# One loading order changed on SyncE: all four quarters of w1 issued right behind the picks

## The reference, cut to what matters

```python
e = stack([tbl_f[ids[:, f]] for f in range(32)], axis=1)      # (512, 32, 32)
x0 = prev = e
for W in (filter_0, filter_1):                                # (1, 32*32, 128), (1, 32*128, 128)
    z = einsum('bhd,bmd->bhmd', x0, prev).reshape(512, h * m, 32)
    prev = relu(einsum('bpd,pn->bnd', z, W[0])); outs.append(prev)
z = sum(concatenate(outs, axis=1), axis=-1)                   # (512, 256)
h = concatenate([z, dense_ctx], axis=1)                       # (512, 272)
h = maximum(h @ W_top1 + b_top1, 0)
h = maximum(h @ W_top2 + b_top2, 0)
y = h @ W_top3                                                # (512, 1)
```

## Time and profile before

| | |
|---|---|
| median of 3 runs | 834.16 us (834.12 to 834.23) |
| the profiled execution | 833.78 us |
| its span (first to last instruction) | 832.0 us |
| PE busy | 825.9 us (99%) |
| ACT busy | 795.8 us (96%) |
| DVE busy | 789.3 us (95%) |
| POOL busy | 731.0 us (88%) |

### The profile page before, as it was taken

One profiled execution on the slowest core, in us unless ns is written; L12 is line 12 of the kernel. 1 busy time (PEld: TensorE's weight loads), 2 busy tenths in 40 slices (PEclk: granted clock), 3 DMA queues, 4 the chain that ended last, 5 costly groups with the idle time before them and its releaser, 6 DMA issues.

```text
span 832.0 us, 15690 instructions
## 1 busy us (share of the span) xinstructions
PE 825.9 (99%) x3627; PEld 677.7 (81%) x3627; DVE 789.3 (95%) x2061; ACT 795.8 (96%) x2808; POOL 731.0 (88%) x550
## 2 busy tenths in 40 slices
PE   8999999999999999999999999999999999999999
PEld 6688888888888888888888888888888888888887
DVE  7799999999999999999999999999999999999996
ACT  4799999999999999999999999999999999999995
POOL 5898999989999999999999999999999999999860
PEclk9999999999999999999999999999999999999999
DMA  5541222221233221132331132221122222122000
GB/s 149 180 143 32 66 81 85 86 85 36 63 82 84 84 86 47 51 85 82 84 87 49 48 87 80 84 86 55 43 87 80 86 85 68 33 83 78 1 13 2
DMA packets 62024, 60.91 MB, mean 73 GB/s; under 512 B 26059, under 2 KB 36939, under 8 KB 61934
## 3 DMA queue, kind: packets, MB, share of 16 engines
q1 hardware_dynamic: 57838, 57.80, 23.4%
q0 software_dynamic: 4096, 2.11, 1.6%
HBM read 55.51 MB, written 4.31 MB: 72 GB/s over the span
## 4 chain that ended last, share of the span: by engine, by line
PE 97%; DMA 1%; POOL 1%; issue 0%; SPq 0%; DVE 0%; ACT 0%
PE ps_y L915 28%; PE ps_y L923 28%; PE ps_y L916 28%; PE ps_c L898 3%; PE ps_c L897 3%; PE ps_c L896 3%; POOL gat L452 1%; PE ps_c L894 1%; DMA w_raw<-w 1%; PE ps_c L885 0%; DMA gat<-table,rows 0%; PE ps_y L1019 0%; DMA ids_and_bounds_sb<-ids_and_bounds 0%; POOL w_lo L459 0%; PE ps_y L1021 0%
## 5 line engine op out<-in xcount | busy, mean ns | idle before, releaser
L571 ACT ACTIVATE prod<-ps_y,es 128x128 f32<-128x128 f32 x2560 | 754.1, 647 | 15.8 <-PE ps_y L923 15.6
L740 DVE SCALAR_TENSOR_TENSOR prod<-ps_y,es,prod 128x128 f32<-128x128 f32 x1536 | 422.6, 340 | 28.7 <-PE ps_y L923 26.4
L915 PE MATMUL ps_y<-w_hi,c_both 128*128 128x512 f32 x1024 | 402.8, 393 | 1.0 <-POOL w_lo L459 1.0
L923 PE MATMUL ps_y<-w_hi,c_both 128*128 128x512 f32 x1024 | 398.8, 390 | 0.0
L916 PE MATMUL ps_y<-w_lo,c_both 128*128 128x512 f32 x1024 | 398.6, 389 | 0.0
L441 POOL TENSOR_TENSOR prod<-prod 128x768 f32<-128x768 f32 x128 | 247.1, 1931 | 45.9 <-DVE prod L740 34.2
L752 DVE TENSOR_REDUCE csum<-prod 128x64 f32<-128x896 f32 x256 | 276.5, 1081 | 0.1
L916 PEld LDWEIGHTS ps_y<-w_lo,c_both 128*128 128x128 f32 x1024 | 192.4, 188 | 43.2 <-issue 1.0
L915 PEld LDWEIGHTS ps_y<-w_hi,c_both 128*128 128x128 f32 x1024 | 192.5, 188 | 42.9 <-issue 2.8
L923 PEld LDWEIGHTS ps_y<-w_hi,c_both 128*128 128x128 f32 x1024 | 192.2, 188 | 41.4
L431 POOL TENSOR_TENSOR z<-first,second 128x512 f32<-128x512 f32 x155 | 199.7, 1299 | 0.1
(11 more groups left out here) (122 smaller groups left out, 295.7 us busy)
## 6 DMA issues: line engine op xcount, KB each, us to landing
second<-et_scratch SPq DMA_DIRECT2D x155, 256.0 KB, 4.8
first<-et_scratch SPq DMA_DIRECT2D x31, 256.0 KB, 3.2
et_scratch<-gat SPq DMA_DIRECT2D x62, 64.0 KB
w_raw<-w SPq DMA_DIRECT2D x4, 512.0 KB, 4.7
h_scratch<-h_sums SPq DMA_DIRECT2D x120, 2.0 KB
gat<-table,rows_now POOLq DMA_INDIRECT x116, 2.4
wt_sb<-wt SPq DMA_DIRECT2D x2, 512.0 KB
rows_now<-rows SPq DMA_DIRECT2D x29, 2.0 KB, 1.7
```

The source lines that it names most:

```text
L571: last = nc.scalar.activation(prod[:, buffer_of(g, u), place // 2, :, place % 2], ps_y[:, bank_of(g, u, k), j * N:(j + 1) * N], ACT.Copy, ...
L740: last = nc.vector.scalar_tensor_tensor(out=summed, in0=ps_y[:, bank_of(g, u, k), j * N:(j + 1) * N], scalar=es[:, g.r, u, h:h + 1], in1=s ...
L915: nc.tensor.matmul(out, hi, w_hi, start=True, stop=False)
L923: nc.tensor.matmul(out, lo, w_hi, start=False, stop=True).then_inc(y_ready, 1)
```

## The change

SP no longer waits for the gathers of group 0. It issues quarters 0 to 3 of `w1` one behind the other right behind the picks. The quarter 3 that stood between the writes and the reads of group 1 is gone from there. The same DMAs are issued in all.

```diff
@@ -317,12 +317,10 @@
             sp.dma_start(w0b_sb, w0b).then_inc(w0_in, 16)
             sp.dma_start(copy_sb[:, :], copy_of).then_inc(w0_in, 16)
             sp.dma_start(picks_sb[:, :, :], picks).then_inc(picks_in, 16)
-            filters(0)
+            for n in range(W1_LOADS):
+                filters(n)
             for s in range(SLOTS):
                 sp.sem_inc(h1_written[s], 16 * BT)
-            sp.wait_ge(gathered[0], 16 * TG)
-            for n in range(1, W1_LOADS - 1):
-                filters(n)
 
             def stage(g):
 
@@ -359,7 +357,6 @@
 
             send(Group(0, 1))
-            filters(W1_LOADS - 1)
             fetch(Group(0, 1))
```

## The result

The change made the kernel slower: 837.53 us in the median of 16 runs (835.41 to 845.12) against 833.96 for the kernel before (833.63 to 834.36, 16 runs). The ratio is 1.0051, with a 95% interval of 1.0032 to 1.0069. The median lies 0.5 us above the range of the prediction (833.7 to 837.0), and what was forecast was +0.8 us, no measurable change. Every ratio in this document leaves out runs in a slower state; only the run at 846.94 us, in one of the experiments, was such a run.

| mean granted clock | runs | us |
|---|---|---|
| 1.000 | 3 | 835.41 to 836.01 |
| 0.997 and 0.998 | 8 | 836.80 to 837.80 |
| 0.996 | 3 | 838.24 to 838.56 |
| 0.994 | 2 | 845.02 and 845.12 |

What follows compares the result with a forecast made beforehand. The prediction took one long PE stream and its start to bound the kernel. Gathers later by 2.0 us less 1.17 us for the removed wait gave +0.8 us, 835.0 us in the median, range 833.7 to 837.0.

Steps and rivals of the forecast that it cites:

- What bounds the kernel: Whole span: one long PE stream with a start in front; moving the start or opening a hole moves the end equally.
- Removed: ACT's wait for quarter 3: At banks 6 and 7 of `w1`: ACT and POOL come sooner, PE's hole shrinks to 0.2 us; gain 1.17 us.
- Moved: 1.5 MB of traffic, onto the gathers: Before the picks: group 0's fourth gather lands at 12.6 instead of 10.6 us, a cost of 2.0 us.
- the round robin: Group 0's gathers, rival: they pass between the quarters, waiting for one packet only; sum -0.3 to -1.2 us, chance 15%.
- my rule: Group 0's gathers: one behind quarters lands when they are through, 0.1 us before the last to 0.6 behind it.
- PE's clock falls in the longer pause: Rival, between warm-up and picks: a 3.6 us pause drops the clock, +2.0 us more, 837.0 us; chance 20%.

Runs made afterwards that it cites:

- the run at 846.94 us: Kernel before with only quarter 3 moved, and DVE instead of POOL making bank 6's `w_lo`: median 839.60 us, ratio 1.0043; the profiled run took 846.94.
- the kernels with quarter 3 moved and the gap: Kernel before with quarter 3 moved, POOL waiting for DVE before its first folds: 833.59 us; with DVE taking bank 6, 833.11; with POOL's `w_lo` held back, 833.48.
- the kernel with one quarter fewer: Kernel before with quarters 0 to 2 issued right behind the picks and quarter 3 behind group 0's gathers: 836.24 us, ratio 1.0012.

## Why the prediction was wrong, point by point

*What bounds the kernel* was right: all of the loss in the profile arises in the first 31 us (+4.70) and is carried to the end (+4.6).

*"Removed: ACT's wait for quarter 3", -1.17 us*: mis-sized. The wait went, but the gain was 0.55. I took POOL's 2.52 us for a fixed length. Counted from the rectify of tile 0, POOL starts at 26.72 - 21.38 = 5.34 us instead of 22.93 - 16.13 = 6.80, so 1.46 sooner and right behind its last gather. There its first subtraction runs into two of DVE's (`w_lo` of bank 5 and the `z_lo` of the other tiles) and takes 2.18 us instead of 1.28, and 0.9 of the 1.46 are lost again. With those kept apart it is 1.28, but POOL then has to start later, and the gain is 9.46 - 9.12 = 0.34. Neither way gives 1.17: what bounds POOL next is the end of DVE's work.

*"Moved: 1.5 MB of traffic, onto the gathers", +2.0 us*: right that the traffic delays the gathers, 2.54 in size. The fourth gather, the one that counts, did land when the quarters ahead were through (13.1 against quarter 3's 12.9). The last quarter came at 12.9 and not at 12.1: quarter 0 already took 5.5 us instead of 5.0, and why the rest took longer too is not shown. A gather that waits for one packet only, as I had read the round robin, was not what decided: with two and three quarters more the delay was 1.6 and 2.5 us. But my rule did not hold as a rule either: the second gather, issued at 5.5 us behind all four quarters, landed at 11.7, 1.2 us before quarter 3, and the third, issued at 6.7, at 12.0. So the order is neither one packet's wait nor first come, first served. That the fourth gather came right behind quarter 3 is in part luck for the rule.

*These two terms alone* make 2.54 - 0.55 = +2.0. The three runs of the changed kernel at full clock were +1.4 to +2.1, and the run with the longer warm-up +1.5. That is already more than twice the +0.8 forecast, but would still lie inside the range.

*"PE's clock falls in the longer pause"*: this is the step at which the prediction failed. In the sum the fall of the clock stood at nothing, as a rival with 20%; 13 of 16 runs had it, and it put the median outside the range. I had named the place and the pause but treated the fall as an unlikely event because the trace before showed no pause between 1.6 us and the start. The pause was even shorter than the 3.6 us I had for it (3.04), since the warm-up matmuls did not end at 10.45 us but at 11.59. The kernel with 16 warm-up matmuls shows the fall at 4.2 us in every run, the one with 23 at 2.5 us in most, and the changed kernel with 42 seldom (2 of 11). The price was put at 2.0 us and was 2.71 in the profiled execution, where all 12 picks ran at the lower level (12 x 0.20 = 2.4, and the small matmuls behind them), and about 1.6 in the eight runs at 0.997 and 0.998 (837.3 in their middle against 835.7 at full clock).

*Not foreseen*: the runs at 845. They are 7 us above the three at 0.996 with a clock that is hardly lower. One blocked subtraction of DVE costs about that, by the trace of the run at 846.94. Runs some 7 us too long appear also with only quarter 3 moved (2 of 12) and now and then in the kernel before (841.4 and 842.0 among 35 runs), and in none of the 34 runs of the kernels with quarter 3 moved and the gap. That it was the cause in the changed kernel's two runs is likely, but no trace of such a run exists, so it stays argued and not shown. Why moving DVE's 0.7 us at 22 us makes it so frequent is open too; in the two traces shown the difference is which of the two engines is ahead some 28 us later.

## What to carry to other kernels

A transfer moved ahead is moved in front of everything issued after it, and here the small gathers on the critical path paid for the large load that had time: hold a bulk load back until the small transfer that starts the compute has landed, and then issue all of it at once (0.55 us in the profile here, by itself not clear of the noise in the runs). When a change makes PE's first wait longer, price the clock as the likely case and fill the wait with warm-up matmuls. When an instruction on POOL starts sooner, look at which two-input instructions of DVE it will now run beside.

## What the runs showed of the hardware that I had not expected

- With a pause ahead of the picks of 2.5 and 3.0 us in the profiled execution, after 8 and 10 us of work, the mean granted clock was below 1.0 in 6 of 10 and 13 of 16 runs, and the same programs ran at 1.0 in the others. The profiled execution of the kernel with one quarter fewer had 2.5 us and stayed at 1.00; with 23 warm-up matmuls it had 2.5 us, and the clock fell to 0.50 only after the picks had begun.
- The 32 warm-up matmuls took 9.00 us in one profiled execution and 10.13 and 10.02 in others.
- A DVE subtraction of two SBUF operands took 6.79 us instead of 0.68 beside POOL instructions without a gap, PE's clock fell to 0.50 in the wait, and together it cost near 7 us; and one POOL subtraction 2.18 us instead of 1.28 beside two of DVE's.
- A hole in the PE stream that waits for a transfer with a fixed landing time absorbs part of a later start: of 2.09 us only 1.54 reached the stream behind it.
